# A fused conditioning and gated FFN on one core: steps by half for three tiles instead of two, part of the weight rounding moved to GpSimd, the first selection tree moved to SBUF

## The reference, cut to what matters

```python
def cond(x, subjects, weights, bias):           # x (32, 32, 256)
    out = jnp.einsum('bct,bcd->bdt', x, weights[subjects])
    return out + bias[subjects][:, :, None]
def qmm(x, w, scale):
    wq = w.astype(jnp.float8_e4m3fn).astype(x.dtype)
    return jnp.einsum('bsi,io->bso', x, wq) * scale
def ffn(h, ...):                                # gate, up (256, 768), down (768, 256)
    gate = jax.nn.silu(qmm(h, gate_w, gate_scale))
    return qmm(gate * qmm(h, up_w, up_scale), down_w, down_scale)
out = x + ffn(cond(x, ...), ...)
```

## Time and profile before

| | before |
|---|---|
| median of 3 runs | 50.0 us |
| profiled execution, whole | 50.52 us |
| its span, first to last instruction | 48.6 us |
| TensorE matmuls busy | 43.6 us |
| VectorE busy | 39.0 us |
| ScalarE busy | 26.3 us |
| GpSimd busy | 9.8 us |

### The profile page before, as it was taken

The page is one execution under the profiler, slowest core; times in us unless marked ns, Lnnn a source line. Parts: engine busy times, 40 slices in busy tenths (PEclk is TensorE's granted clock), DMA queues, the critical chain, the costliest instruction groups (busy, mean ns, idle before and its releaser), DMA issues.

```text
span 48.6 us, 678 instructions
## 1 busy us (share of the span) xinstructions
PE 43.6 (90%) x201; PEld 33.6 (69%) x201; DVE 39.0 (80%) x74; ACT 26.3 (54%) x45; POOL 9.8 (20%) x19
## 2 busy tenths in 40 slices
PE   1999899999999999999999999999999999998000
PEld 1331499997788878888788887888878888976000
DVE  2828899699899999899998999997659495985900
ACT  0945406984559684597319695631845728870000
POOL 3028904049910003930000000000000000370000
PEclk9999999999999999999999999999999999999997
DMA  0499999999950000000000000000000000028093
GB/s 0 101 316 391 357 390 379 416 410 414 410 223 7 0 0 0 0 0 0 0 0 13 7 0 0 0 0 0 0 0 0 0 0 7 0 89 332 10 333 99
DMA packets 2995, 5.71 MB, mean 118 GB/s; under 512 B 432, under 2 KB 1072, under 8 KB 2992
## 3 DMA queue, kind: packets, MB, share of 16 engines
q1 hardware_dynamic: 2704, 5.53, 30.9%
q10 hardware_dynamic: 288, 0.15, 1.1%
HBM read 4.63 MB, written 1.05 MB: 117 GB/s over the span
## 4 chain that ended last, share of the span: by engine, by line
PE 81%; DMA 5%; POOL 3%; DVE 2%; issue 1%; DVEq 1%; POOLq 0%
PE gu L552 46%; PE acc L560 23%; PE acc L525 8%; DMA const_in<-in_consts_dram 5%; PE acc L516 3%; DVE res L454 2%; POOL bias_tok L327 2%; DVEq L70 1%; POOL bias_r L320 1%; POOL bias_r L318 0%; POOLq L323 0%; POOLq L317 0%
## 5 line engine op out<-in xcount | busy, mean ns | idle before, releaser
L552 PE MATMUL gu<-h_hi,w_q 128*128 128x512 f32 (+1 forms) x52 | 15.2, 378 | 0.0
L552 PE MATMUL gu<-h_lo,w_q 128*128 128x512 f32 (+1 forms) x52 | 15.1, 377 | 0.0
L281 ACT CAST f_hi<-fuse 128x512 fp32r<-128x512 f32 (+1 forms) x13 | 7.6, 587 | 10.5 <-DVE fuse L441 10.5
L449 DVE TENSOR_TENSOR f_lo<-fuse,f_hi 128x512 fp32r<-128x512 f32 (+1 forms) x13 | 8.8, 675 | 3.2 <-ACT f_hi L281 3.2
L552 PEld LDWEIGHTS gu<-h_hi,w_q 128*128 128x128 f32 x52 | 9.5, 187 | 2.1
L552 PEld LDWEIGHTS gu<-h_lo,w_q 128*128 128x128 f32 x52 | 9.4, 187 | 2.2 <-DVE h_lo L421 0.2
L441 DVE SCALAR_TENSOR_TENSOR fuse<-gu,const_in,silu 128x512 f32<-128x512 f32 (+1 forms) x13 | 9.2, 706 | 0.4 <-ACT silu L274 0.4
L274 ACT ACTIVATE silu<-gu,const_in 128x512 f32<-128x512 f32 (+1 forms) x13 | 8.5, 651 | 1.1 <-PE gu L552 1.1
L560 PE MATMUL acc<-f_lo,w_q 128*128 128x512 f32 (+1 forms) x26 | 8.0, 381 | 0.0
L560 PE MATMUL acc<-f_hi,w_q 128*128 128x512 f32 (+1 forms) x26 | 7.8, 376 | 0.0
L239 ACT ACTIVATE w_big<-w_big,big_least 128x768 f32<-128x768 f32 (+2 forms) x8 | 6.2, 770 | 0.5 <-DVE w_big L358 0.5
(11 more groups left out here) (37 smaller groups left out, 24.7 us busy)
## 6 DMA issues: line engine op xcount, KB each, us to landing
w_in<-in_weights_dram SPq DMA_DIRECT2D x4, 384.0 KB, 6.2
x_tok<-in_x_by_time_dram SPq DMA_DIRECT2D x1, 1024.0 KB, 8.9
out_dram<-res SPq DMA_DIRECT2D x3, 256.0 KB, 2.1
x_sb<-in_x_dram SPq DMA_DIRECT2D x1, 512.0 KB, 3.6
w_in<-in_weights_dram SPq DMA_DIRECT2D x2, 256.0 KB, 4.0
x_sb<-in_x_dram SPq DMA_DIRECT2D x2, 256.0 KB, 4.2
w_in<-in_weights_dram SPq DMA_DIRECT2D x2, 128.0 KB, 4.9
const_in<-in_consts_dram SPq DMA_DIRECT2D x1, 151.0 KB, 2.4
```

The costliest lines, as they stand in the source:

```text
L281: nc.scalar.copy(f_hi[:, s % SLOTS, cols], fuse[:, s % SLOTS, cols]).then_inc(f_hi_made, 1)
L449: nc.vector.tensor_tensor(f_lo[:, s % SLOTS, cols], fuse[:, s % SLOTS, cols], f_hi[:, s % SLOTS, cols].bitcast(F32), ALU.subtract).then_in ...
L552: last = nc.tensor.matmul(gu[:, (s + q) % 2, part, cols], w_q[:, i, col:col + P], h[:, n, k, cols], start=(v == 0 and k == 0), stop=(v == ...
```

## The change

- `STEP`: tiles 0 to 2 come with both halves in turn (steps 0 to 5), then tiles 3, 4, 5 with half 0 (steps 6 to 8), then with half 1 (9 to 11). So tile 4 is first used in step 7 instead of 8, tile 5 in step 8 instead of 9.
- Rounding: GpSimd adds and subtracts the whole of tile 3 (768 columns) and the down columns of tiles 4 and 5 as well; VectorE is left with gate and up of tiles 4 and 5. `power` and `big` of (1, down) come ahead of tile 2's. On VectorE the later passes move to other steps, on ScalarE `big` of tile 3 to step 2, of tile 4 to step 3, of tile 5 to step 5.
- Head: both trees lie in SBUF; the first copy of `tree[0]` is made by ScalarE for three pairs and by GpSimd for the fourth; the high part of the bias is made by VectorE. The second copy of the bits goes. GpSimd places the first half's bias, then a block of the first half, then the second half's bias. For the first half, block copies go one to ScalarE, one to GpSimd, two to VectorE.
- Tail: `down(8)` is moved into the last part and signals when half 0 of each block is complete, and VectorE finishes both blocks of half 0 in step 10, between `fuse_of(10)` and `rest_of(10)`. `y_sc` and GpSimd's add go. Both pieces of `gate_up(11)` follow each other; the last down matmuls are ordered so that block 0 of half 1 is complete four half-width matmuls ahead of block 1. `both(s, b)` is the high and the low matmul of step s for block b; `high(b, q)` and `low(b, q)` are those of piece q of step 11.

```diff
@@ -47,8 +47,10 @@
-    STEP = [(i, n) for i in range(IC - 2) for n in range(HALVES)] + [(i, n) for n in range(HALVES)
-                                                                     for i in range(IC - 2, IC)]
+    BY_HALF = 3
+    STEP = [(i, n) for i in range(IC - BY_HALF) for n in range(HALVES)] + [(i, n) for n in range(HALVES)
+                                                                           for i in range(IC - BY_HALF, IC)]
     assert TOK == 512 and B * C == G * P and weights.shape[2] == WCOL
...
@@ -157,21 +156,19 @@
-        BIGS = ((0, 0, GU), (1, 0, GU), (0, GU, WCOL), (2, 0, WCOL), (1, GU, WCOL)) + tuple((i, 0, WCOL) for i in range(3, IC))
-        DVE_PIECES = ((0, 0, GU), (0, GU, WCOL), (2, 0, WCOL)) + tuple((i, 0, WCOL) for i in range(3, IC))
-        POOL_PIECES = ((1, 0, GU // 2), (1, GU // 2, GU), (1, GU, WCOL))
-        ACT_BLOCKS = ((0, 1), (0,))
-        POOL_BLOCKS = ((), (1, 2))
+        BIGS = ((0, 0, GU), (1, 0, GU), (0, GU, WCOL), (1, GU, WCOL), (2, 0, WCOL)) + tuple((i, 0, WCOL) for i in range(3, IC))
+        DVE_PIECES = ((0, 0, GU), (0, GU, WCOL), (2, 0, WCOL), (4, 0, GU), (5, 0, GU))
+        POOL_PIECES = ((1, 0, GU // 2), (1, GU // 2, GU), (1, GU, WCOL), (3, 0, WCOL), (4, GU, WCOL), (5, GU, WCOL))
+        ACT_BLOCKS = ((0,), (0,))
+        POOL_BLOCKS = ((1,), (1, 2))
         DVE_BLOCKS = ((2, 3), (3,))
...
@@ -242,9 +238,10 @@
             act.wait_ge(const_ld, 16)
-            for n in range(HALVES):
-                nc.scalar.copy(tree[n], cond_rep[:, :, 0].unsqueeze(2).to_broadcast([P, PAIRS, GH, D])
-                               ).then_inc(tree_even[n], 1)
+            nc.scalar.copy(tree[0][:, 0:PAIRS - 1], cond_rep[:, 0:PAIRS - 1, 0].unsqueeze(2).to_broadcast([P, PAIRS - 1, GH, D])
+                           ).then_inc(tree_even[0], 1)
+            nc.scalar.copy(tree[1], cond_rep[:, :, 0].unsqueeze(2).to_broadcast([P, PAIRS, GH, D])
+                           ).then_inc(tree_even[1], 1)
...
@@ -286,22 +283,22 @@
                     continue
-                if s <= 3:
-                    big(s + 2)
-                elif s in (5, 6):
-                    big(s + 1)
+                if s == 1:
+                    big(3)
+                    big(4)
+                elif s in (2, 3):
+                    big(s + 3)
+                elif s == 5:
+                    big(7)
                 round_of(s)
...
             s = STEPS - 1
-            silu_of(s, 0, PIECES[0])
-            act.wait_ge(y0_made, 1)
-            nc.scalar.activation(y_sc[:], acc[:, 0], ACT.Copy, scale=down_col[:, 0:1]).then_inc(y_scaled, 1)
-            silu_of(s, 1, PIECES[1])
+            for q in range(LAST):
+                silu_of(s, q, PIECES[q])
             for q in range(LAST):
                 round_of(s, q, PIECES[q])
-            act.wait_ge(res_dve, 3)
-            act.dma_start(out_rows[:, 1, TOK:TOK + TOK // 2], res[:, 1, 1, 0:TOK // 2]).then_inc(stored, 16)
+            act.wait_ge(res_dve, 4)
+            act.dma_start(out_rows[:, 1, TOK:TOK + TOK // 2], res[:, 1, 1, PIECES[0]]).then_inc(stored, 16)
...
@@ -312,32 +309,39 @@
             pool.wait_ge(const_ld, 16)
-            nc.gpsimd.tensor_copy(bias_r[:], bias_in).then_inc(bias_hi_made, 1)
+            nc.gpsimd.tensor_copy(tree[0][:, PAIRS - 1], cond_rep[:, PAIRS - 1, 0].unsqueeze(1).to_broadcast([P, GH, D])
+                                  ).then_inc(tree_even_pool, 1)
+            pool.wait_ge(tree_even_pool, 1)
+            def place(n):
+                pool.wait_ge(tree_level[n], BITS)
+                for j in POOL_BLOCKS[n]:
+                    nc.gpsimd.tensor_copy(*block_of(n, j)).then_inc(cond_placed[n], 1)
+                pool.wait_ge(cond_placed[n], J)
...
             pool.wait_ge(bias_lo_made, 1)
...
-            for n in range(HALVES):
-                place_bias(n)
+            place_bias(0)
             pool.wait_ge(bd_zeroed, 1)
-            pool.wait_ge(bias_placed, HALVES)
-            pool.wait_ge(tree_level[1], BITS)
-            for j in POOL_BLOCKS[1]:
-                nc.gpsimd.tensor_copy(*block_of(1, j)).then_inc(cond_placed[1], 1)
-            pool.wait_ge(cond_placed[1], J)
+            pool.wait_ge(bias_placed, 1)
+            place(0)
+            place_bias(1)
+            pool.wait_ge(bias_placed, 2)
+            place(1)
...
@@ -450,50 +452,47 @@
                     power(0, GU, WCOL)
+                    power(1, GU, WCOL)
                     power(2)
...
                 elif s == 2:
-                    power(3)
+                    power(4)
                 elif s == 3:
...
                 elif s == 4:
-                    power(4)
+                    take_big(3)
                 elif s == 5:
                     add_big(4)
-                elif s == 6:
-                    add_big(5)
+                elif s == STEPS - 2:
+                    dve.wait_ge(x_tok_ld, 16)
+                    for b in range(TB):
+                        dve.wait_ge(y0_made, b + 1)
+                        finish(0, b)
                 rest_of(s)
...
                 elif s == 1:
-                    power(1, GU, WCOL)
+                    power(3)
                     take_big(2)
                 elif s == 3:
-                    take_big(3)
-                elif s == 4:
                     power(5)
...
                     take_big(4)
-                elif s == 6:
-                    take_big(5)
...
             s = STEPS - 1
-            fuse_of(s, 0, PIECES[0])
-            dve.wait_ge(x_tok_ld, 16)
-            dve.wait_ge(y0_made, 2)
-            finish(0, 1)
-            fuse_of(s, 1, PIECES[1])
+            for q in range(LAST):
+                fuse_of(s, q, PIECES[q])
             for q in range(LAST):
...
@@ -571,34 +570,48 @@
                 gate_up(s)
-                if s >= LAG:
+                if LAG <= s < STEPS - 2:
                     down(s - LAG)
...
             s = STEPS - 1
-            for i in (IC - 2, IC - 1):
+            def both(s, b):
+                down_block(s, 0, b)
+                return down_block(s, 1, b)
+            def high(b, q):
+                pe.wait_ge(f_hi_made, s + q + 1)
+                down_block(s, 0, b, PIECES[q])
+            def low(b, q):
+                pe.wait_ge(f_lo_made, s + q + 1)
+                return down_block(s, 1, b, PIECES[q])
+            for i in range(IC - BY_HALF, IC):
                 wait_quant(pe, i, GU)
-            gate_up(s, 0, PIECES[0])
-            pe.wait_ge(f_hi_made, s - 1)
+            pe.wait_ge(f_lo_made, s - 2)
+            for b in range(TB):
+                both(s - 3, b).then_inc(y0_made, 1)
+            for q in range(LAST):
+                gate_up(s, q, PIECES[q])
             pe.wait_ge(f_lo_made, s - 1)
-            for b in range(TB):
-                down_block(s - 2, 0, b)
-                down_block(s - 2, 1, b).then_inc(y0_made, 1)
-            gate_up(s, 1, PIECES[1])
-            for v, part_made in enumerate((f_hi_made, f_lo_made)):
-                pe.wait_ge(part_made, s)
-                for b in range(TB):
-                    down_block(s - 1, v, b)
+            both(s - 2, 0)
+            pe.wait_ge(f_lo_made, s)
+            both(s - 1, 0)
+            both(s - 2, 1)
+            high(0, 0)
+            low(0, 0)
+            both(s - 1, 1)
+            high(0, 1)
+            low(0, 1).then_inc(y1_made, 1)
             for q in range(LAST):
-                pe.wait_ge(f_hi_made, s + q + 1)
-                for b in range(TB):
-                    down_block(s, 0, b, PIECES[q])
-                pe.wait_ge(f_lo_made, s + q + 1)
-                for b in range(TB):
-                    last = down_block(s, 1, b, PIECES[q])
-                    if q == LAST - 1:
-                        last.then_inc(y1_made, 1)
+                high(1, q)
+                last = low(1, q)
+            last.then_inc(y1_made, 1)
```

49 lines of the change are left out of this document (21 added, 28 removed).

## The result

The changed kernel took 52.17 and 52.19 us, against 50.11 for the kernel before (median of four): 1.039 times as long (ratio of the means), 95% interval 1.025 to 1.053. Two more executions of it, at a lower granted clock (0.967), took 53.4 us and are left out of every comparison. The forecast was 50.8 with a range to 51.8: the sign was right, the size wrong, and the time lies outside the range.

What follows compares the result with a forecast made beforehand. TensorE's gapless matmul chain was taken as the bound. Middle +1.25, tail -0.40 and head -0.05 gave +0.8 us on a median of 50.0, so 50.8 us, with an 8-in-10 range of 49.4 to 51.8.

Steps and rivals of the forecast that it cites:

- The bound and the sign: TensorE's gapless chain from 10.84 to 44.61 us bounds the kernel; its middle can only lengthen by waits; total +0.8 us.
- The middle: Steps between head and tail: TensorE waits on rounding and the shared port, 0.07 + 1.05 + 0.13 = +1.25 us.
- Tile 2 "just fits": Steps 1 and 2: `take_big(2)` ends near 19.75 us, tile 2 is loaded at 19.87, so no stall there.
- Rival 2: Middle: GpSimd wins each gap between two VectorE operations; middle near +3, total 52.2 us; chance 0.10.
- `rest(2)` waits until 22.5: At `down(2)`: GpSimd's tile 3 add delays `rest(2)`, `f_lo(2)` ends at 23.1; TensorE loses 1.05 us with an exposed load.
- All that comes behind it: Middle after `down(2)`: 0.13 us at `down(3)`, then 256-column pieces cost VectorE at most 0.6 each, absorbed by slack.
- rival 1: Middle: port blocking stays off the path, costing 0.07; total 49.6 us; against it, 14.9 of 14 us port time; chance 0.36.
- the order of steps: Middle: tiles 4 and 5, needed a step earlier, are done at 27.8 and 31.0, wanted at 29.6 and 32.4.
- The tail: From `down(8)` on: `finish(1,0)` starts earlier, so the last `finish` ends at 7.00 instead of 7.40; -0.40 us.
- The head: Before `gate_up(0)`: earlier select and blocks against a later bias; -0.05 us, bounds -0.15 and +0.1.
- the moment at which TensorE doubles its pace: Head: a shift of when TensorE gets fast would move the total by a tenth or two either way.
- The chances: Whole kernel: forecast 0.42, rivals 0.36, 0.10 and 0.12; faster 0.37, same 0.13, slower 0.50.

Runs made afterwards that it cites:

- e10: Changed kernel with GpSimd's subtract (not add) of tile 3 held until `f_lo(2)` is made; 52.70 us, ratio 1.046 to the kernel before.
- e1: Changed kernel with GpSimd's add and subtract of tile 3 cut into three pieces of 256 columns each; 50.68 us, ratio 1.011 to the kernel before.
- e7: Changed kernel with the weight rounding and its passes as before, leaving the new order by half, head and end; 51.30 us, ratio 1.021.
- e6: Kernel before with another end only: both halves of `gate_up(11)` in succession, half 0 finished behind the last `rest`; 50.19 us, ratio 1.002.
- e5: Kernel before with the changed head alone (trees in SBUF, bias order, shared blocks); 50.04 us, ratio 0.997.
- e8: Kernel before with only tile 3's add and subtract moved to GpSimd, 768 columns each; 50.78 us, ratio 1.010.
- e2: Changed kernel with GpSimd's add of tile 3 held until `f_lo(2)` is made; 52.52 us, ratio 1.049 to the kernel before.

## Why the prediction was wrong, point by point

**The bound and the sign: right.** TensorE's chain without gaps, no matmul removed, the loss as a wait of `acc`'s weight loads for `f_lo` near 22 us, by the port that GpSimd and VectorE share. The 768-wide instruction takes 1.85 us, as scaled from 256 and 512 columns, and blocks for its whole length.

**The middle: +1.25 forecast, +2.60 measured, and this is the miss.** Three of its terms:
- Tile 2 "just fits": it was 0.29 late, 0.37 with its exposed load, where the forecast had 0.07 for all of this. `f_lo(1)` was blocked for 0.54 us by the subtract of the down columns of tile 1. Rival 2 had this step, and its sign, a weight load of `gu` that waits for tile 2 at 20 us, came true.
- "`rest(2)` waits until 22.5": it waited for two GpSimd instructions and not for one, since the subtract, already waiting, got the port when `power(4)` let go of it. 2.26 us instead of 1.05. Rival 2 again, in its mechanism and its place; its total of 52.2 is what was measured, in part by luck, with a middle of +3 where +2.6 was found, but I gave it 0.10.
- All that comes behind it, 0.13 forecast. In the changed kernel this was even right (0), because the large stall had given VectorE time.

So the step that failed is "`rest(2)` waits until 22.5": one GpSimd instruction ahead of it, and 1.05 us, where there were two, and 2.26. But the order in which the port is granted isn't the whole cause. In e10 GpSimd couldn't get in between, the stall at `down(2)` was near that of my timeline, and the time was no better: 52.7. The deeper fault is that I followed one collision and took what came behind it as nearly free, although I had written the balance down myself under rival 1: 14.9 us of port time asked for in 14. GpSimd takes 1.85 us to add 768 columns and VectorE 0.95, so each column moved to GpSimd holds the port twice as long as it did. VectorE was spared 2.9 us and blocked for 4.7 (0.2 before), a net 1.6 us, on an engine with hardly any idle time in these steps.

The balance alone doesn't give the time either. In e1 the same columns in pieces of 256 ask for no less of the port, and the middle is +1.25, which is the forecast's number, but not by its path. And the order of steps, which the forecast priced at nothing because tiles 4 and 5 would be ready, costs 1.95 by itself (e7). That no wait of the changed kernel is for tile 4 or 5 doesn't speak against this: by then TensorE was already 2.6 us late. How the 2.60 divide depends on the path by which one takes the change apart.

**The tail: -0.40 forecast, -0.25 in the profile, -0.38 in e1 and -0.48 in e7.** The size was right. The reason I gave, that block 0 is complete earlier, holds: `finish(1,0)` starts 0.16 us ahead of the last matmul's start. What I didn't ask is what the stores need. In e6 the last `finish` came 0.6 us earlier, and the stores, now all at the end, took it all.

**The head: -0.05 forecast, -0.53 in the profile, -0.15 (0 to -0.3) in e5.** I had the moment at which TensorE doubles its pace as a thing that might upset the head, by "a tenth or two"; `gate_up(0)` moves with it by up to 0.5 us between profiles of one head. The granted clock that I read from the first slice on was no reading ahead of 7.02 us, as e5 says. I also had the sign that the profile of before was a late one (50.52 against 50.0) and did not use it.

With the measured terms the sum closes in medians: 50.1 + 2.6 - 0.25 - 0.15 = 52.3, against 52.2.

**The chances.** Slower had the largest chance, 0.50; one outcome can't say whether that was fair. The range ended below rival 2's 52.2 by my choice of leaving it out.

No kernel tried beats the kernel before by more than the measurement can tell; the head alone (0.997, 0.994 to 1.000) comes nearest.

## What to carry to other kernels

Before elementwise work is moved from VectorE to GpSimd, add up who holds the port that they share: here VectorE's operations with two inputs in SBUF and its `power` passes, and GpSimd's adds and subtracts at nearly twice the time for each column. Where that sum was near the length of the stretch, as in this kernel, the move blocked VectorE for as long as it spared it (e8) or longer (changed, e1), and two other moments for it didn't help (e2, e10). Short instructions did (e1): the longest one sets what a waiting operation loses, and a second one, already queued, blocks VectorE's next operation too. When an offload and a new order of steps come together, run each alone: here the order, which makes tiles due earlier, cost more than the offload. And where a sum finds one stall, ask for the balance of the whole stretch before calling the rest free.
